# A gated cross-attention and mixture-of-experts block: four value strips at a time, a slot table by one-hot matmuls, and the keys' high halves on another engine

## What is computed

```python
x = x + tanh(g_xattn) * attention(layernorm(x), ctx, ctx)    # 32 query heads, 8 key/value heads of 16, softmax(q k / 4) v
x = x + tanh(g_ffn) * moe(layernorm(x))

def moe(x):                       # 4096 tokens, 512 features, 7 routed experts and a shared one
    gate = x @ Wr + br
    ids = top_k(gate + gate_bias, 2)
    probs = softmax of gate over the two chosen
    per expert: u = x @ Wup + bup;  g = silu(u @ Wgate + bgate) * u;  eo = g @ Wdown + bdown
    return sum(probs * eo over the two) + shared expert(x)
```

## Time and profile before

| | us |
|---|---|
| median of 3 runs | 1425.33 (1423.9 to 1425.56) |
| the profiled execution | 1424.88 |
| its span, first to last instruction | 1423.1 |
| TensorE busy in the span | 1281.2 (90%) |
| VectorE busy | 900.5 (63%) |
| ScalarE busy | 570.5 (40%) |
| GpSimd busy | 464.2 (33%) |

### The profile page before, as it was taken

The page is one execution under the profiler, slowest core; times in us unless marked ns, Lnnn a source line. Parts: engine busy times, 40 slices in busy tenths (PEclk is TensorE's granted clock), DMA queues, the critical chain, the costliest instruction groups (busy, mean ns, idle before and its releaser), DMA issues.

```text
span 1423.1 us, 32236 instructions
## 1 busy us (share of the span) xinstructions
PE 1281.2 (90%) x11123; PEld 884.8 (62%) x11123; DVE 900.5 (63%) x1670; ACT 570.5 (40%) x1013; POOL 464.2 (33%) x495
## 2 busy tenths in 40 slices
PE   2588888888876889969999999999999999999996
PEld 2244444444435767757777777777777777777773
DVE  5888888888878874425555455544444444446887
ACT  3477777777774422212222222222222222222220
POOL 3255555555536456711111111111111111004454
PEclk8699999999995699989999999999999999999998
DMA  7344333343336835565263453635254621167666
GB/s 259 128 135 134 133 133 133 133 133 133 133 112 215 279 32 61 65 153 191 74 229 111 162 192 120 220 119 198 84 189 140 207 87 59 50 209 238 215 206 192
DMA packets 100764, 213.41 MB, mean 150 GB/s; under 512 B 13776, under 2 KB 14290, under 8 KB 100720
## 3 DMA queue, kind: packets, MB, share of 16 engines
q1 hardware_dynamic: 87408, 176.02, 39.0%
q0 software_dynamic: 13312, 36.82, 8.5%
HBM read 228.30 MB, written 66.13 MB: 207 GB/s over the span
## 4 chain that ended last, share of the span: by engine, by line
PE 56%; issue 4%; POOL 3%; DMA 3%; DVE 0%; POOLq 0%; DVEq 0%
PE PS L1365 35%; PE PS L1384 18%; POOL idd L562 3%; PE PS L1353 3%; DMA idd<-stk,sct 2%; DVE X L1111 0%; DMA idr<-idd 0%; POOL stk L557 0%; POOL sct L556 0%; DVE ob L1111 0%; DVE X L1091 0%; DVE yb L1085 0%; DVEq L66 0%; PE PS L1399 0%; POOLq L565 0%
## 5 line engine op out<-in xcount | busy, mean ns | idle before, releaser
L1384 PE MATMUL PS<-wb,ghl 128*128 128x512 f16 x1296 | 291.9, 382 | 6.8 <-DVE ghl L1077 3.6
L1365 PE MATMUL PS<-xT,wb 128*128 128x256 f16 x2592 | 293.8, 274 | 1.1 <-DVE xT L1055 1.1
L1365 PE MATMUL PS<-uhl,wb 128*128 128x256 f16 x2592 | 293.4, 273 | 1.0 <-DVE uhl L1065 1.0
L1365 PEld LDWEIGHTS PS<-xT,wb 128*128 128x128 f16 x2592 | 254.5, 98 | 31.7 <-issue 1.3
L1365 PEld LDWEIGHTS PS<-uhl,wb 128*128 128x128 f16 x2592 | 252.2, 98 | 30.4 <-DVE uhl L1065 1.3
L1384 PEld LDWEIGHTS PS<-wb,ghl 128*128 128x128 f16 x1296 | 127.5, 98 | 151.3 <-issue 11.9
L741 ACT ACTIVATE sl<-PS,bb 128x256 f32<-128x256 f32 x216 | 90.7, 471 | 208.3 <-PE PS L1365 208.3
L1072 DVE TENSOR_TENSOR g<-sl,u 128x512 f32<-128x512 f32 x108 | 74.7, 691 | 157.2 <-ACT sl L741 154.4
L839 DVE TENSOR_REDUCE negm<-PS 128x4 f16<-128x512 f32 x256 | 163.3, 678 | 11.6 <-PE PS L1206 11.4
L732 ACT ACTIVATE u<-PS,bb 128x256 f32<-128x256 f32 x216 | 90.7, 471 | 196.0 <-PE PS L1365 171.9
L721 ACT ACTIVATE xT<-PS 128x1024 f16<-128x1024 f16 x54 | 55.3, 1024 | 278.1 <-PE PS L1353 273.3
(11 more groups left out here) (148 smaller groups left out, 1472.6 us busy)
## 6 DMA issues: line engine op xcount, KB each, us to landing
wb<-wsc SPq DMA_DIRECT2D x126, 1024.0 KB
wst<-in_wall SPq DMA_DIRECT2D x32, 768.0 KB, 5.6
wsc<-whl SPq DMA_DIRECT2D x32, 768.0 KB, 4.2
ysl<-yb SPq DMA_DIRECT2D x46, 512.0 KB
bd<-in_bdown SPq DMA_DIRECT2D x42, 256.0 KB
X<-in_x SPq DMA_DIRECT2D x8, 1024.0 KB, 7.6
xnd<-xhl SPq DMA_DIRECT2D x32, 256.0 KB, 2.2
xs<-xnd SPq DMA_DIRECT2D x32, 256.0 KB
```

The costliest lines, as they stand in the source:

```text
L1365: ins = pe.matmul(bank[:, hf, (m % 2) * TT:(m % 2 + 1) * TT], wb[:, par, l, k, w, m * P:(m + 1) * P], rhs(x, k), start=(n == 0), stop=(n = ...
L1384: ins = pe.matmul(PS[2][:, t, :], ghl[:, x, k, t * P:(t + 1) * P], wb[:, par, 2, k, w, :], start=(n == 0), stop=(n == len(TERMS) - 1))
```

## The change

Three things. `outputs` is called once per two units and issues four strips one after another (32 columns each); `pv_done` then counts twice per batch. The two copies of the keys' high halves move from ScalarE's `high` into GpSimd's `split_kq`, ahead of the key split, with a wait for its own result. The scatter goes: VectorE makes from each slot number its low 7 bits and the rest, and in tiles 2 to 5, between `split_u` and `down_out`, writes per token group a one-hot row of 128 and a one-hot column of 76 times the token's number (8 batches per tile, 32 instructions); at tile 6 TensorE multiplies 64 such pairs and sums them in PSUM, which is the table already transposed. Numbers are shifted by 2048 so that f16 holds them exactly. VectorE's loop over tiles 2 to 5 is unrolled.

```diff
@@ -417,6 +419,8 @@
             for par in range(2):
                 sp.wait_ge(y_out[par], 16 * (SH_A // 2))
 
+            sp.wait_ge(S["idx_ready"], 3)
+
             def early_row(n, par):
...
             def split_kq(half, par, quad):
                 b = 2 * half + par
+
+                need(g, S["pv_done"], 2 * (b - 3))
+                g.nop(nofuse=True)
+                ck = C[:, bass.ds(b, 1), :].rearrange("p o (h d) -> p (o h) d", d=D)
+                for dup in range(2):
+                    ins = g.tensor_copy(kcat[:, quad, :, dup, 0:3:2, :], ck.unsqueeze(2).to_broadcast([P, NKV, 2, D]))
+                ins.then_inc(S["kh_ready"], 1)
                 g.wait_ge(S["kh_ready"], b + 1)
+                g.nop(nofuse=True)
...
                 after = follow(half, par, quad, 2)
+                if isinstance(half, int) and number(half, par) == 0:
+                    g.wait_ge(c_in[1], 16)
                 if after is not None:
                     split_kq(*after)
...
-            g.wait_ge(S["idz"], 16)
-            g.wait_ge(S["rt_pos"], 1)
-            g.wait_ge(S["id_ready"], 7)
-
-            def scatter(h, first):
...
-            scatter(0, True)
-            with g.Fori(1, NB // SB // 2) as h:
-                scatter(h, False)
-            for j in range(2):
-                g.wait_ge(scat[j], 16 * NB)
-            g.dma_start(idr[:, :], idd.rearrange("(c p) o -> c (p o)", p=P)).then_inc(S["id_load"], 16)
...
             def high(half, par, quad):
                 b = 2 * half + par
 
-                need(act, S["pv_done"], UNITS * (b - 3))
-                cv = C[:, bass.ds(b, 1), :].rearrange("p o (h d) -> p (o h) d", d=D)
-                for dup in range(2):
-                    ins = act.activation(kcat[:, quad, :, dup, 0:3:2, :], cv.unsqueeze(2).to_broadcast([P, NKV, 2, D]), ACT.Copy)
-                ins.then_inc(S["kh_ready"], 1)
...
-                need(act, S["pv_done"], n - 3)
+                need(act, S["pv_done"], 2 * (2 * half + par) + u // 2 - 1)
...
-                v.tensor_copy(rpos[:, :, :].rearrange("p b k -> p k b"), sel[:, :, :]).then_inc(S["rt_pos"], 1)
+                link(v.tensor_copy(slot_i[:, 0, :, :], sel[:, :, :]))
+                link(v.tensor_scalar(slot_i[:, 1, :, :], slot_i[:, 0, :, :], P - 1, None, ALU.bitwise_and))
+                link(v.tensor_scalar(slot_i[:, 2, :, :], slot_i[:, 0, :, :], P.bit_length() - 1, None, ALU.logical_shift_right))
+                link(v.tensor_copy(slot_f[:, :, :, :], slot_i[:, 1:3, :, :]))
                 return ends
+
+            def one_hots(bs):
+
+                for k in range(2):
+                    for b in bs:
+                        v.tensor_scalar(row1h[:, k, b, :], lane[:, :], slot_f[:, 0, k, b:b + 1], None, ALU.is_equal)
+                        ins = v.tensor_scalar(col1h[:, k, b, :], lane[:, 0:R_COLS], slot_f[:, 1, k, b:b + 1], tok[:, b:b + 1],
+                                              ALU.is_equal, ALU.mult)
+                ins.then_inc(S["hot_ready"], 1)
...
                 if not last:
                     split_u(i + 1, 1 - par)
+                if hots is not None:
+                    one_hots(hots)
...
-            def outputs(half, par, quad, u):
-                b = 2 * half + par
-                pe.wait_ge(S["exp_done"], 2 * (UNITS * b + u + 1))
+            def outputs(half, par, quad, hf):
+                b = 2 * half + par
+                pe.wait_ge(S["exp_done"], 2 * (UNITS * b + 2 * hf + 2))
                 pe.wait_ge(S["va_ready"], b + 1)
-                if u % 2 == 0:
-                    need(pe, S["oT_ready"], 2 * b + u // 2)
-                for kv in range(2):
-                    c = (u % 2) * 2 + kv
+                need(pe, S["oT_ready"], 2 * b + hf)
+                for c in range(4):
+                    u, kv = 2 * hf + c // 2, c % 2
...
                     tr_o(*pv[:2], 0)
-                    outputs(*pv, 2)
                 tr_neg(half, par, 1)
                 step(half, par, 1, nx and (*nx[:2], 0))
                 if not start:
-                    outputs(*pv, 3)
+                    outputs(*pv, 1)
                 if nx is not None:
                     tr_q(*nx[:2], 1)
                 step(half, par, 2, nx and (*nx[:2], 1))
                 if not start:
                     tr_o(*pv[:2], 1)
-                outputs(half, par, quad, 0)
                 if nx is not None:
                     tr_neg(*nx[:2], 0)
                 step(half, par, 3, nx and (*nx[:2], 2))
-                outputs(half, par, quad, 1)
+                outputs(half, par, quad, 0)
...
-                    pe.wait_ge(S["id_load"], 16)
                     pe.wait_ge(S["y_ready"], 2 * i)
-                    pe.transpose(PS[2][:, 0, 0:R_COLS], idr[:, :], id32[0:R_COLS, 0:R_COLS]).then_inc(S["idT"], 1)
+                    pe.wait_ge(S["hot_ready"], HOT_TILES)
+                    pairs = [(k, b) for k in range(2) for b in range(NB)]
+                    for n, (k, b) in enumerate(pairs):
+                        ins = pe.matmul(PS[2][:, 0, 0:R_COLS], row1h[:, k, b, :], col1h[:, k, b, :],
+                                        start=(n == 0), stop=(n == len(pairs) - 1))
+                    ins.then_inc(S["idT"], 1)
```

More of the change, by code:

```diff
@@ L48 @@
 EARLY = NB * SH_A // SH_TILES
-SB = 4
+HOT_TILES = SH_A - 4
+MID = NB * P // 2
 XC = 8
@@ L135, in program @@
             rnk = sm("rnk", [P, NB, 8], F32)
+        with ExitStack() as third:
+            row1h = sb("row1h", [P, 2, NB, P], F16, third)
+            col1h = sb("col1h", [P, 2, NB, R_COLS], F16, third)
         yg = sb("yg", [P, 4, 2, HID], F32)
@@ L544, in _ @@
                 low2(i)
-            g.wait_ge(S["idz"], 16)
-            g.wait_ge(S["rt_pos"], 1)
-            g.wait_ge(S["id_ready"], 7)
-            def scatter(h, first):
-                for j in range(2):
-                    if not first:
-                        g.wait_ge(scat[j], 16 * 2 * SB * h)
-                        g.nop(nofuse=True)
-                    g.tensor_copy(sct[:, j, :, :], rpos[:, bass.ds((2 * h + j) * SB, SB), :]).then_inc(S["sct_ready"], 1)
-                    g.tensor_copy(stk[:, j, :], tok[:, bass.ds((2 * h + j) * SB, SB)]).then_inc(S["sct_ready"], 1)
-                    g.wait_ge(S["sct_ready"], 4 * h + 2 * j + 2)
-                    g.nop(nofuse=True)
-                    for b in range(SB):
-                        for k in range(2):
-                            g.indirect_dma_start(out=idd, out_offset=bass.IndirectOffsetOnAxis(ap=sct[:, j, b, k:k + 1], axis=0),
-                                                 in_=stk[:, j, b:b + 1], in_offset=None).then_inc(scat[j], 16)
-            scatter(0, True)
-            with g.Fori(1, NB // SB // 2) as h:
-                scatter(h, False)
-            for j in range(2):
-                g.wait_ge(scat[j], 16 * NB)
-            g.dma_start(idr[:, :], idd.rearrange("(c p) o -> c (p o)", p=P)).then_inc(S["id_load"], 16)
             for j in range(4):
@@ L974, in choose @@
             def choose():
-                v.wait_ge(S["id_ready"], 7)
+                v.wait_ge(S["id_ready"], 8)
                 for k in range(2):
@@ L1116, in _, with tile @@
             split_u(0, 0)
-            def tile(half, par, stored, early=None, late=None):
+            def tile(half, par, stored, early=None, late=None, hots=None):
                 i = 2 * half + par
@@ L1145, in _ @@
                 tile(0, par, 0)
-            with v.Fori(1, SH_A // 2 - 1) as h:
+            for j in range(4):
+                v.wait_ge(x2_out[j], 16 * (NB // 4))
+            for h in range(1, SH_A // 2 - 1):
                 for par in range(2):
-                    tile(h, par, h)
+                    n = NB // HOT_TILES
+                    c = 2 * (h - 1) + par
+                    tile(h, par, h, hots=range(c * n, c * n + n))
             v.wait_ge(S["idT"], 1)
-            v.tensor_copy(idx[:, :], PS[2][:, 0, 0:R_COLS]).then_inc(S["idx_ready"], 1)
+            v.tensor_scalar(idx[:, :], PS[2][:, 0, 0:R_COLS], float(MID), None, ALU.add).then_inc(S["idx_ready"], 1)
             for par in range(2):
@@ L1296, in body @@
                 step(half, par, 3, nx and (*nx[:2], 2))
-                outputs(half, par, quad, 1)
+                outputs(half, par, quad, 0)
             over_batches(pe, body)
             tr_o(NB // 2 - 1, 1, 0)
-            for u in range(2, UNITS):
-                outputs(NB // 2 - 1, 1, NB % 4 + 3, u)
+            outputs(NB // 2 - 1, 1, NB % 4 + 3, 1)
             tr_o(NB // 2 - 1, 1, 1)
```

17 lines of the change are left out of this document (7 added, 10 removed).

## The result

The changed kernel takes 1489.35 us (median of 4 runs, 1482.2 to 1493.11) against 1424.62 us for the kernel before on the same chip: 1.045 times as long, 95% interval 1.0413 to 1.0488. The forecast was 1441 us, the range 1424 to 1470. The direction was right, the size wrong, and the time is outside the range. The profiled execution took 1493.11 us, its span is 1491.3 us, 68.2 longer than before.

A forecast was written before the change was run, and what follows sets the result against it. The prediction took attention to be bound by a cycle of VectorE and the chain over GpSimd, 11.71 us per period. Terms +26.6 + 0.65 - 10.6 - 0.6 = +16.05 on 1424.88 give 1440.9, said as 1441 us; range 1424 to 1470.

The forecast's parts named there:

- The cycle: Attention loop: `att` over GpSimd to the maximum 4.48 us, from there to `att` 7.23 us, together the whole 11.71 us period.
- The keys' high halves: Attention, GpSimd's `split_kq`: two copies and a wait add 0.95 us per period, 28 times, +26.6 us (16.8 to 42.8).
- The wait for all of `ctx`: GpSimd's first body in attention: put at nothing; if the load lands later, it costs what it is later.
- The four strips: Attention, TensorE: 2.06 us less work per batch, idling longer ahead of `tr_neg`; worth nothing, 0 to 0.6 us lost.
- rival C: Attention loop: the four strips don't run side by side, 28 x 1.03 = 29 us more, 1470 us; chance 3%.
- Rival B: Attention: TensorE falls to half clock (1.2 GHz), 28 x 2.3 = 64 us more, 1505 us; chance 5%.
- The table: Expert tiles: tile 6's gate layer delay falls from 17.26 to 6.7 us, gain 10.6 us (6.7 to 13.8).
- The wait of tile 6: Tile 6: TensorE waits 2.78 us for tile 5's `y`, behind one-hots at 0.14 us each, 4.5 us per tile.
- The 64 matmuls: Tile 6, TensorE: accumulating matmuls of 76 columns at 0.045 us each, 2.9 us together.
- `place()`: Ahead of the first `gating`: three more small chained instructions, +0.65 us (0.4 to 0.9).
- The one-hots of tiles 2 to 4: VectorE, tiles 2 to 4: evacuation of `y` some 2 us later, no cost; at 0.24 us each, 2.1 us.
- Tile 4's tokens: Tile 4: with the scatters gone, TensorE's 1.18 us wait for tokens may shrink, -0.6 us (0 to -1.2).

The follow-up runs named there:

- both fills: Changed kernel plus strips of constants at TensorE's two waits for GpSimd and in the two old places of the strips: 1448.09 us.
- the run with table and order: Kernel before with only the one-hot table and GpSimd's key and query splits put ahead of the residual: 1410.52 us, ratio 0.958.
- keys alone, strips of constants: Kernel before with keys' high halves on GpSimd, plus strips of constants put at TensorE's two waits for GpSimd: 1507.82 us.
- the splits early: Changed kernel with keys' high halves back on ScalarE and GpSimd's splits ahead of the residual: 1428.96 us, ratio 0.9652.

## Why the prediction was right or wrong

**The cycle.** Right. The chain from `att` over GpSimd to the maximum sets the period; at full clock, what was added to it came out in full (12.64 us with both fills). That it is only 0.2 us ahead of the next one (the run with table and order) was not seen.

**The keys' high halves.** Right: 0.95 us forecast, 0.88 measured (2.11 against 1.23 us) and 12.64 - 11.72 = 0.92 per period at full clock. Two copies in 0.73 us, the wait 0.15. The wait for all of `ctx` cost nothing: in the changed kernel `tr_k` of batch 3 starts only 0.3 us late.

**The four strips.** The row was right: eight instructions in 1.06 us at full clock, so rival C is out. With the two places filled again the period is 12.64 us, and with the pairs (keys alone, strips of constants) 12.6: grouping four strips is worth nothing in itself, as was said. The step "TensorE then idles longer there ... Worth: nothing" failed by its second half. The idling was priced by the path only and not by the clock: alone, it cost 0.3 us per period, and 0.7 with the splits early.

**Rival B, the clock.** Here the prediction failed. It named the mechanism, gave TensorE's busy share after the change as 65%, worked out what half clock would cost, and then gave it 5% with "I think that the wide matmuls that are left keep the clock up". No row supported that sentence. What the runs showed in its place: where waits of 1.0 and 0.7 us, or of 1.1 and 1.4 us, stand in one period, the clock falls to half for part of it in every period or every second one, wide strips or not (the wide strips then take 1.93 us for 1.06); in the changed kernel it is granted 0.74 over the loop. The price was somewhat low: 2.3 us per period forecast for half clock throughout, 14.21 - 12.64 = 1.57 measured with 0.74, which in proportion would be 3.0 at 0.50 (an estimate from these numbers). Rival B also was all or nothing. A clock that goes up and down gives times between the 1441 us of the one case and the 1505 of the other; the measured one lies there, and the range had ended at 1470. So it is partly luck that rival B's 1505 lies near the 1489 measured: too low a price, for a state that was taken to last throughout.

The sentence of the Trainium skill that the prediction cited ("TensorE: Matmul & The Clock Gate", Part 1) was weighed too lightly: taking busy time away while adding idle time did work against the change. The same page describes, under "A second HAM failure mode: psum-queue depth-cycling", a kernel in which short idle stretches between groups of matmuls made the clock go up and down; this case agrees, with a clock of 1.00, 0.70, 0.50 in neighbouring windows of 2 us.

**Tail of attention and norm.** Put at nothing, measured +5.6 us: the last batches and the strips behind them (1.93 us at 475.87) have the half clock too. In the run with both fills this stretch is 97.6 us, against 96.9 before.

**The table.** Direction right, size too large: with `place()` and tile 4's tokens 7.45 us were gained in place of 10.55, and at tile 6 alone 17.26 - 9.46 = 7.8 in place of 10.6. The wait of tile 6: the one-hots follow each other in 0.16 and 0.21 us, 0.187 in the mean, not 0.14, so 6.0 us per tile, and y is done 1.3 us later than forecast: a wait of 4.11 us, where 2.78 was said. The 64 matmuls came out of this wait at half clock, as the window shows: 4.04 us for 2.9, and the transposes 1.3 for 1.0. Sum 9.46 us for 6.7: the clock again in most of the rest. `place()`: 0.65 us forecast, 4.27 - 3.60 = 0.67 measured. The one-hots of tiles 2 to 4 cost nothing (16.55 us between gate layers), as forecast. Tile 4's tokens came in time: 1.35 us gained for 0.6, over the bound of 1.2. Another 1.2 us were lost over the later tiles; no step had them.

**The chances.** Slower had 83% and was right. The range missed because the fall of the clock, which the profile after shows in its first line, had 5% and nothing of the range.

## What to carry to other kernels

Before taking work off TensorE in a loop that isn't bound by it, look at what it will wait for instead: here waits of 1.0 and 0.7 us in a period of 12, where 0.2 and 0.7 had stood, were enough to lose the full clock in every period, 1.1 us alone was not, and the slowed matmuls then lay on the path. An engine's idle time "costs nothing" only if its clock stays; a forecast should price the half-clock case from rows at both levels and let it hold for part of the time. And the cheap test is to fill the wait with work whose result is thrown away: if the kernel gets faster, it was the clock.

## What the runs showed of the hardware

**More work, less time.** The changed kernel with eight more strips of constants per period has TensorE busy 286.62 of 310 us and a period of 12.64 us; without them it is busy 232.53 of 299 us on the first chip, and the period is 14.21 us (14.52 on another).

**On some chips TensorE is held up while GpSimd issues its 64 small scatters.** On all three further chips the kernel before takes 1472 to 1478 us, against 1424.6 on the first. On the one where it was traced its attention is the same (11.73 us, clock 1.00), and the time goes in tiles 1 and 2, while GpSimd issues its scatters. Windows of the kernel before on that chip, and then on the first, same stretch:

```profile
535.00:590.00 55.00, 20.97 (x62) 6.57 (x60) 4.05 (x7) 2.27 (x6) 40.49 (x50) 0.56 0.02 1
```

```profile
535.00:590.00 55.00, 53.82 (x454) 41.48 (x452) 25.49 (x41) 14.62 (x30) 39.62 (x46) 1.00 0.59 66
```

GpSimd does the same in both, TensorE 62 matmuls in place of 454. None waits for data; the timeline of that chip puts the idle time down to issue:

```profile
588.32 0.37 PE L1365 MATMUL PS<-uhl,wb 128*128 128x256 f16 x1 [1.82 <-issue]
589.03 0.38 PE L1365 MATMUL PS<-uhl,wb 128*128 128x256 f16 x1 [0.34 <-issue]
591.12 0.37 PE L1365 MATMUL PS<-uhl,wb 128*128 128x256 f16 x1 [1.71 <-issue]
592.51 0.37 PE L1365 MATMUL PS<-uhl,wb 128*128 128x256 f16 x1 [1.02 <-issue]
```

They start one by one, 0.71, 2.09 and 1.39 us apart, near multiples of 0.70 us. The kernels with the strips alone, the keys alone and the keys with holds have it too (80.1, 83.3 and 82.3 us between the gate layers of tiles 1 and 2), and none of those without scatters has it (16.6 us). So where the table alone was measured it is worth 58.5 us (1474.94 - 1416.43), and on the first chip 7.5. That the scatters do it is shown by their removal, together with the rest of the table's change; by which way they hold up TensorE's instructions, and why not on the first chip, stays open.
